# Attention over heads on one Trainium2 core: two tiles of 128 tokens softened with one set of operations

## The reference

```python
qkv = jnp.einsum('bsm,mhd->bshd', x, Wqkv) + bqkv        # 16 heads, 48 = 3 x 16
q, k, v = jnp.split(qkv, 3, axis=-1)                     # [b, s, h, 16]: seq_len = q.shape[-2] = 16 heads
scores = jnp.einsum('...hqd,...hkd->...hqk', qb, kb) / jnp.sqrt(jnp.float32(d))
scores = jnp.where(mask == 0, -1000000000.0, scores)     # mask: lower triangle over the heads
w = jax.nn.softmax(scores, axis=-1)
ob = jnp.einsum('...hqk,...hvd->...hqd', w, vb)          # k and v are separate labels
y = jnp.einsum('bshd,hdm->bsm', attn, Wout) + bout
```

## Time and profile before

| what | value |
|---|---|
| time, median of 3 runs | 434.84 us (433.45 to 437.3) |
| the profiled execution's own time | 432.32 us |
| its span in the profile | 430.5 us |
| mean granted TensorE clock | 0.96 of full speed |
| instructions | 6336 |

### The profile page before, as it was taken

How to read it: one execution, slowest core, us unless ns; L and a number is a source line. 1 busy time by engine, 2 the same in 40 slices (tenths; PEclk the granted TensorE clock), 3 DMA queues, 4 the chain that set the end, 5 groups by cost and what they waited for, 6 DMA issues and landing times.

```text
span 430.5 us, 6336 instructions
## 1 busy us (share of the span) xinstructions
PE 385.0 (89%) x2132; PEld 185.6 (43%) x2132; DVE 320.1 (74%) x503; ACT 233.1 (54%) x444; POOL 149.6 (35%) x159
## 2 busy tenths in 40 slices
PE   2999797989999999999999999898798688977696
PEld 1645342222222222222222354676576356545475
DVE  6638699888878888788887244577689989899643
ACT  2146232667776777868777865533254153553332
POOL 4024305997000000000000001345668678967143
PEclk9999897999999999999999999999899979898889
DMA  7608993950000000000000000000000000000001
GB/s 208 226 3 210 246 249 62 181 106 2 0 3 0 1 0 1 0 1 0 1 0 2 1 2 2 2 2 0 2 1 2 0 0 2 24 0 2 24 2 49
DMA packets 12644, 17.42 MB, mean 40 GB/s; under 512 B 4391, under 2 KB 10443, under 8 KB 11950
## 3 DMA queue, kind: packets, MB, share of 16 engines
q1 hardware_dynamic: 10862, 15.95, 15.3%
q10 hardware_dynamic: 1760, 1.18, 0.9%
HBM read 12.73 MB, written 4.19 MB: 39 GB/s over the span
## 4 chain that ended last, share of the span: by engine, by line
PE 65%; DVE 19%; ACT 5%; DMA 4%; issue 4%; POOL 1%; SPq 1%; ACTq 0%; DVEq 0%
PE ps L1223 15%; PE ps L1209 13%; PE ps L1185 12%; PE ps L1356 7%; DVE s_wide L1034 3%; PE ps L1345 3%; DVE xn L892 3%; DVE mx L931 2%; PE ps L1330 2%; PE ps L1131 2%; DVE pack L1023 2%; DVE stats L875 2%; DMA pack<-q_parts 2%; ACT pbuf L781 1%; PE ps L1391 1%
## 5 line engine op out<-in xcount | busy, mean ns | idle before, releaser
L931 DVE TENSOR_REDUCE mx<-ps 128x1 f32<-128x1024 f32 x128 | 151.0, 1220 | 30.5 <-PE ps L1185 29.8
L781 ACT ACTIVATE pbuf<-ps 128x512 f32<-128x512 f32 x256 | 135.8, 603 | 52.3 <-PE ps L1209 51.5
L1185 PE MATMUL ps<-pack 112*128 (+1 forms) x256 | 79.1, 392 | 4.6 <-DMA pack<-q_parts 2.7
L1209 PE MATMUL ps<-pack 115*128 (+1 forms) x256 | 81.8, 386 | 0.8 <-ACT pbuf L781 0.8
L620 POOL TENSOR_TENSOR rstd<-rstd,minus_half 128x2 f32<-128x2 f32 x16 | 12.1, 756 | 192.8 <-DVE rstd L882 192.7
L1223 PE MATMUL ps<-pbuf,v_slot 128*32 128x512 f32 x512 | 68.2, 604 | 2.0 <-ACT pbuf L781 0.9
L1209 PEld LDWEIGHTS ps<-pack 115*128 (+1 forms) x256 | 21.2, 97 | 80.6 <-issue 60.9
L1356 PE MATMUL ps<-w_nat,pack 128*128 128x256 bf16 x384 | 54.1, 288 | 1.8 <-POOL pack L657 1.8
L669 POOL TENSOR_TENSOR pbuf<-wT 128x1024 f32<-128x1024 f32 (+3 forms) x32 | 49.8, 1574 | 8.4 <-ACT wT L832 8.4
L657 POOL TENSOR_TENSOR pack<-pack 128x256 bf16<-128x256 f32 x64 | 42.0, 666 | 24.2 <-DVE pack L1023 24.2
L1023 DVE TENSOR_TENSOR pack<-pack 128x256 f32<-128x256 f32 x64 | 35.1, 556 | 16.8 <-ACT pack L826 16.6
(11 more groups left out here) (112 smaller groups left out, 383.2 us busy)
## 6 DMA issues: line engine op xcount, KB each, us to landing
pack<-q_parts SPq DMA_DIRECT2D x6, 384.0 KB, 13.9
w_nat<-in_L_ffn_w_dram SPq DMA_DIRECT2D x2, 1024.0 KB, 6.6
k_parts<-parts SPq DMA_DIRECT2D x2, 768.0 KB, 7.4
q_parts<-parts SPq DMA_DIRECT2D x4, 384.0 KB, 9.0
pack<-k_parts SPq DMA_DIRECT2D x4, 384.0 KB, 7.2
pack<-k_parts SPq DMA_DIRECT2D x2, 768.0 KB, 9.1
x_res<-in_L_attn_a_x_dram SPq DMA_DIRECT2D x4, 256.0 KB, 3.6
out_dram<-x_res SPq DMA_DIRECT2D x4, 256.0 KB, 2.1
```

The lines of the kernel that those rows point to most:

```text
L781: act.activation(pbuf[:, c % 2, j, :], ps[:, b, :], ACT.Exp).then_inc(drained[b], 1)
L931: dve.tensor_reduce(mx[:, par, k:k + 1], ps[:, b:b + 2, :].rearrange("p b k -> p (b k)"), AX_X, ALU.max) \
L1185: ins = pe.matmul(ps[:, b + n, :], q_group[0:ROWS, qh, at, j, P * qt:P * qt + P].rearrange("p g t -> p (g t)"), k_group[0:ROWS, at, j, HAL ...
L1209: pe.matmul(ps[:, b, :], k_group[0:SROWS, at, j, P * c:P * c + P].rearrange("p g t -> p (g t)"), q_group[0:SROWS, qh, at, j, :].rearrange( ...
```

## The change

Tiles 2p and 2p + 1 are softened together. The steps vs, soft, exp_heads and wv exist once for each pair p, in the planned place of the odd tile, with operations over both tiles: the mask over 128 numbers, maximum, subtraction, exp, sum and outer product over 512, reciprocal and product over 32. vs.p computes both tiles' summed values, in one bank, with the same matmuls as before. o, o_out, bo_y and res stay per tile; those of the even tile move to directly before those of the odd tile, 0.9 apart in the plan. The planned start of tile 6 moves from 81.69 to 84.0 and that of tile 7 from 89.69 to 90.5. The first sum of each even tile from tile 2 on also waits until the last pair has been shifted, a semaphore of VectorE's own; the qk copy waits for GpSimd's products of tile t - 3 instead of that tile's drained bank.

In the sorted list TensorE's part becomes, for example: qk.5, bo_y.3, two y_parts, lnt.3.1, y.1.0, qk.6, h.1.1.0, vs.2, h.1.1.1, h.1.1.2, qk.7, h.1.1.3, o.4, and later vs.3, y.1.1, o.6, h.1.2.0, o.7, bo_y.6, bo_y.7, h.1.2.1, h.1.2.2, lnt.3.3.

```diff
-HEADS_AT = (39.0, 47.93, 56.72, 63.93, 72.93, 78.84, 81.69, 89.69)
-HEADS_LAG = (0.0, 2.7, 8.6, 9.89, 11.1, 11.36, 13.07, 13.77, 14.1, 15.1)
+HEADS_AT = (39.0, 47.93, 56.72, 63.93, 72.93, 78.84, 84.0, 90.5)
+HEADS_LAG = (0.0, 2.7)
+SOFT_LAG = (8.6, 9.89, 11.1, 11.36)
+HEADS_OUT_LAG = (13.07, 13.77, 14.1, 15.1)
+HEADS_OUT_STEP = 0.9
...
         if t % 2:
-            yield from pair_slots(3, t // 2, at + HEADS_LAG[-1])
+            p = t // 2
+            for lag, kind in zip(SOFT_LAG, ("vs", "soft", "exp_heads", "wv")):
+                yield at + lag, (kind, p)
+            for i in (0, 1):
+                for lag, event in zip(HEADS_OUT_LAG, (("o", "b", 2 * p + i), ("o_out", "b", 2 * p + i), ("bo_y", 2 * p + i),
+                                                      ("res", 2, 2 * p + i))):
+                    yield at + lag + HEADS_OUT_STEP * i, event
+            yield from pair_slots(3, p, at + HEADS_OUT_LAG[-1] + HEADS_OUT_STEP)
...
             def qk_out(t):
                 if t >= 3:
-                    is_drained(act, ("vs", t - 3))
+                    act.wait_ge(products, QUADS * (t - 2))
...
-            def exp_heads(t):
-                act.wait_ge(shifted, t + 1)
-                act.activation(probs[:, t % 2, :, :], probs[:, t % 2, :, :], ACT.Exp, scale=SCALE).then_inc(exped, 1)
+            def exp_heads(p):
+                act.wait_ge(shifted, p + 1)
+                act.activation(probs, probs, ACT.Exp, scale=SCALE).then_inc(exped, 1)
...
                 dve.wait_ge(products, taken[0])
+                if quad == QUADS - 1 and t and t % 2 == 0:
+                    dve.wait_ge(shifted, t // 2)
...
+            def soften(p):
 
                 dve.wait_ge(reduced, taken[0])
+                is_filled(dve, ("vs", p))
+                hmax = beside_v_sums(p, 1)
+                link(dve.tensor_tensor(s_diag, s_diag, causal[:, :, :].unsqueeze(1).broadcast_to([P, 2 * QUADS, 4, 4]), ALU.add))
+                link(dve.tensor_reduce(hmax, s_raw, AX_X, ALU.max))
+                dve.tensor_tensor(probs, s_raw, hmax.unsqueeze(3).broadcast_to([P, 2, H, H]), ALU.subtract).then_inc(shifted, 1)
+
+            def head_outputs(p):
+
+
+                dve.wait_ge(exped, p + 1)
+                hsum = beside_v_sums(p, 2)
+                link(dve.tensor_reduce(hsum, probs, AX_X, ALU.add))
+                link(dve.reciprocal(w_sum[:, :, :], hsum))
+                link(dve.tensor_tensor(w_sum[:, :, :], hsum, w_sum[:, :, :], ALU.mult))
+                n = number["o", "b", 2 * p]
+                for i in (0, 1):
+                    is_filled(dve, outs[n - 2 + i])
+                dve.tensor_tensor(o_norm.rearrange("p r (h n) -> p r h n", h=H),
+                                  w_sum[:, :, :].unsqueeze(3).broadcast_to([P, 2, H, HD]),
+                                  beside_v_sums(p, 0).unsqueeze(2).broadcast_to([P, 2, H, HD]), ALU.mult) \
+                    .then_inc(drain_sem(("vs", p)), 1)
...
                 else:
-                    is_drained(pe, ("vs", t))
+                    is_drained(pe, ("vs", t // 2))
...
+            def heads_v_sums(key):
+
+                p = key[1]
+                if p == 0:
                     pe.wait_ge(vsum_ready, 1)
+                to_fill(pe, key)
+                for i in (0, 1):
+                    t, out = 2 * p + i, beside_v_sums(p, 0)[:, i, :]
+                    pe.matmul(out, ones[0:1, :], b_vsum[:, :], start=True, stop=False)
+                    for d in range(DC):
+                        ins = pe.matmul(out, xT[:, d, P * t:P * t + P], w_vsum[:, d, :], start=False, stop=(d == DC - 1))
                 ins.then_inc(fill_sem(key), 1)
```

More of the change, by code:

```diff
@@ L195, in heads_slots @@
     for t, at in enumerate(HEADS_AT):
[L196 to L199, removed]
+        for lag, kind in zip(HEADS_LAG, ("qk", "qk_out")):
+            yield at + lag, (kind, t)
         for n in range(QUADS):
@@ L220, in tail_events @@
     for t in range(TT):
-        assert all(place["sum", t, quad] < place["soft", t] for quad in range(QUADS))
+        for quad in range(QUADS):
+            assert place["sum", t, quad] < place["soft", t // 2]
+            assert t < 2 or place["soft", t // 2 - 1] < place["sum", t, quad]
     for k in (1, 2, 3):
@@ L340, in build @@
         s_raw = s_wide[:, :, 0:H * H].rearrange("p r (i j) -> p r i j", i=H)
-        s_diag = s_wide[:, :, :].rearrange("p r (q x) -> p r q x", q=QUADS)[:, :, :, 0:4 * H] \
-            .rearrange("p r q (i j) -> p r q i j", i=4)[:, :, :, :, 0:4]
+        s_diag = s_wide[:, :, :].rearrange("p r (q x) -> p (r q) x", q=QUADS)[:, :, 0:4 * H] \
+            .rearrange("p q (i j) -> p q i j", i=4)[:, :, :, 0:4]
         w_out = sb("w_out", [P, DC, D])
@@ L371, in build @@
         rsum = sb("rsum", [P, 2, H])
-        w_sum = sb("w_sum", [P, H])
+        w_sum = sb("w_sum", [P, 2, H])
         w_vsum = sb("w_vsum", [P, DC, HD])
@@ L457, in is_filled, with beside_v_sums @@
             return ps[:, b, :]
-        def beside_v_sum(t, n):
-            return ps[:, uses["vs", t][0], HD * n:HD * n + HD]
+        def beside_v_sums(p, n):
+            return ps[:, uses["vs", p][0], 2 * HD * n:2 * HD * n + 2 * HD].rearrange("p (i h) -> p i h", i=2)
         def is_drained(eng, key):
@@ L1032, in head_scores @@
                 dve.wait_ge(products, taken[0])
+                if quad == QUADS - 1 and t and t % 2 == 0:
+                    dve.wait_ge(shifted, t // 2)
                 _, _, terms = factors(t, quad, slot)
                 dve.tensor_reduce(s_raw[:, t % 2, i, 0:nj], terms, AX_X, ALU.add).then_inc(reduced, 1)
-            def soften(t):
+            def soften(p):
                 dve.wait_ge(reduced, taken[0])
[L1039 to L1060, removed]
+                is_filled(dve, ("vs", p))
@@ L1394, in heads_qk @@
                 ins.then_inc(fill_sem(key), 1)
-            def heads_v_sum(key):
-                t = key[1]
-                if t == 0:
+            def heads_v_sums(key):
+                p = key[1]
+                if p == 0:
                     pe.wait_ge(vsum_ready, 1)
[L1401 to L1404, removed]
+                to_fill(pe, key)
[4 more added lines that the diff above has]
+                        ins = pe.matmul(out, xT[:, d, P * t:P * t + P], w_vsum[:, d, :], start=False, stop=(d == DC - 1))
                 ins.then_inc(fill_sem(key), 1)
             tail = {"w": w_transposed, "ao_t": o_to_tokens, "o": o_to_features, "ao_y": project_o,
-                    "lnt": transpose_pair, "h": hidden, "y": ffn_out, "qk": heads_qk, "vs": heads_v_sum,
+                    "lnt": transpose_pair, "h": hidden, "y": ffn_out, "qk": heads_qk, "vs": heads_v_sums,
                     "bo_y": project_o}
```

## The result

The changed kernel is slower: 447.67 us (median of 4 runs, 443.47 to 450.04) against 434.14 us (median of 4), ratio 1.0316 with a 95% interval of 1.0274 to 1.0359. The forecast was 433.8 us with a range of 428.5 to 439.0. The profiled execution took 448.01 us, with a span of 446.2.

What follows compares the result with a forecast made beforehand. TensorE was taken as the bound on average, in the tail waiting mostly for VectorE's layer norms. Step offsets of -0.4 us and -0.6 for a table load made -1.0: from 434.84 to 433.8 us, range 428.5 to 439.

Steps and rivals of the forecast that it cites:

- Saving on VectorE: Softening on VectorE: about 5.5 us less work over four pairs, plus 1 to 2 us from fewer mask stalls.
- ScalarE, 7.7 and 0.8 us: Softening on ScalarE: 7.7 us off through fewer exp and gelu table loads, some 0.8 us from fewer exps.
- Step (a): TensorE up to h.1.0.0 at 345 us: two norms about as before, offset 0, bounds -1.1 and +1.1 us.
- Step (b): TensorE up to lnt.3.1: idle there grows from 1.2 to about 2.6 us; offset +0.4, bounds -1.0 and +2.
- Step (c): TensorE up to o.4: waits some 3 us for the pair's outer product; offset -0.9 us.
- Step (d): TensorE up to lnt.3.2: tile 6's outer-product wait and softening gone, norm hangs on bo_y.5; offset -3.0 us.
- (e): TensorE up to o.6: vs.3 and joint softening longer; offset -1.6 us at the low clock, -2.4 at the high.
- (f): TensorE up to lnt.3.3: more work before the last norm; offset 0.0 at the low clock, -0.8 us at the high.
- bunched output drops the clock: Rival: longer waits at lnt.3.1 and o.4, each followed by the low clock; about +5 us, 440 us; chance 0.13.
- VectorE's saving reaches the end: Rival: tail gains at o.4 and lnt.3.2 last, high clock follows; some -6.3 us, 428.5 us; chance 0.25.
- Joined operations cost double: Rival: operations over 512 numbers cost twice those of 256, VectorE saves only stalls; 434 to 436 us; chance 0.04.
- The two signs of being wrong: Prediction wrong if lnt.3.3 comes 3 us or more before 407.5, or a pair's operations cost what two tiles' did.

Runs made afterwards that it cites:

- experiment 2: Kernel before with only the new starts of tiles 6 and 7 and the changed waits, every tile softened by itself: ratio 1.0011.
- experiment 13: Tiles softened singly in their own places, even outputs directly before odd ones, odd outputs and layer norm where the kernel before has them: ratio 1.0126 to that kernel.
- experiment 5: Tiles softened singly in their own places, even outputs directly before odd ones, odd outputs and layer norm 0.9 later: 447.10 us, ratio 1.0289 to the kernel before.
- experiment 1: Changed kernel's order of steps, but each softening operation done tile by tile over 256 numbers instead of 512: 450.32 us, ratio 1.0392 to the kernel before.
- experiment 6: Changed kernel with both tiles' outputs and the layer norm planned 0.9 earlier, joint softening unchanged: ratio 1.0251 to the kernel before.
- experiment 7: Only tiles 0 and 1 softened jointly, outputs bunched as in the changed kernel, tiles 2 to 7 each by itself: ratio 1.0157 to the kernel before.
- experiment 9: Changed kernel with GpSimd waiting for the normalised pair after one power alone, at norm.3.0: ratio 1.0209 to the kernel before.
- experiment 14: Changed kernel with outputs planned 0.9 earlier and GpSimd waiting for the normalised pair at norm.3.0: ratio 1.0274 to the kernel before.

## Why the prediction was wrong

In steps from the kernel before, each uncertain by 0.4 to 0.8 per cent: new starts 0.1%; even outputs bunched +1.2%, shifted by 0.9 +1.6% (experiments 2, 13, 5); softening of the even tile late +1.0% (experiment 1 against 5); operations joined -0.8% (the change against experiment 1). The steps run from one end to the other, so that they add up to the measured 3.2% proves nothing. They also depend on their order. With the outputs 0.9 earlier, joint softening costs 1.25% (experiment 6 against 13, uncertain by 0.6), with 11.1 us of waits for outer products against 7.4, and not 0.3; and going back by 0.9 gives only 0.65%, not 1.6. What is shown is that the order of the steps costs 3 to 4% (experiments 1 and 5) and that joined operations don't. The savings were sized rightly, the order was not.

- **What bounds it:** read rightly. The large item of TensorE's waits was the norms, and the change made that item 7.8 us larger.
- **Saving on VectorE, 5.5 us and 1 to 2 of stalls:** the operations fell from 22.6 to 16.4 us (the sums of their groups), 6.2 with the mask's stalls. Of single terms, only the reciprocal was off: 0.358 us for 32 numbers against 0.258 for 16, where 0.27 had been taken. But the engine's busy time fell by 1.3 only: stalled norms gave 4.1 us back (L892's group of 18 had 15.2 us, L902's has 19.3).
- **ScalarE, 7.7 and 0.8 us:** 8.2 measured.
- **Step (a), 0 with bounds of 1.1:** this step failed first, by 6.9 us. It took "the two norms about as before" and followed TensorE and VectorE alone; the two copies that change places in ScalarE's list, and the products behind them, stand nowhere in it. norm.3.0 began 4.2 us behind (the second projection, a qk at the low clock with 3.45 us for four matmuls that took 1.98, and norm.2.3 held for 2.57 us instead of 0.74) and then took 2.8 us longer than before. In the profiles with pair 0 shifted by 0.9 and no gate (the changed kernel, experiments 1, 5 and 7) tile 3's copy comes first and the norm takes 4.31 to 4.32 us; in those without it (the kernel before, experiments 2, 6 and 13) it takes 1.55 or 1.56. Why TensorE got the low clock at that qk stays open: the wait ahead of it (1.25 us) is hardly longer than before (1.10).
- **Step (b), +0.4:** +1.1 measured, with 3.04 us of wait where 2.6 had been forecast. Right in kind.
- **Step (c), a gain of 1.3 (from +0.4 to -0.9):** 1.9 gained, right in kind: 3.98 us of wait at o.4 against "some 3".
- **Step (d), -3.0 forecast, a loss of 2.1 instead of a gain of 2.1 from (c) on:** this step failed next. It said that the layer norm then hangs on bo_y.5 and gave that no price. From the start of o.4 to the end of bo_y.5 TensorE took 9.6 us (388.72 to 398.34), where the same matmuls take about 5.9 at the high clock (an estimate from the rows of the kernel before), as the 3.98 us wait was followed by the low one. VectorE, which was to be the engine freed, waited 3.48 and 2.65 us for the two projections meanwhile:

```profile
394.98 0.42 DVE L987 TENSOR_TENSOR x_res<-ps,x_res 128x256 f32<-128x256 f32 x1 [3.48 <-PE ps L1341]
...
398.38 0.42 DVE L987 TENSOR_TENSOR x_res<-ps,x_res 128x256 f32<-128x256 f32 x1 [2.65 <-PE ps L1341]
```

- **Steps (e) and (f), -1.6 and 0:** 2.6 and 4.2 us lost where 1.4 and 1.6 had been forecast. The two projections of 1.13 us each took 2.08 there:

```profile
415.22 2.08 PE L1341 MATMUL ps<-w_out,parts 128*128 128x256 f32 x4
...
417.55 2.08 PE L1341 MATMUL ps<-w_out,parts 128*128 128x256 f32 x4
```

- **The rivals:** "bunched output drops the clock" was the nearest, with 0.13 of chance, but its 440 us are still 7.7 short. It named the two waits, and both came; but it charged them once each and saw no wait ahead of lnt.3.0. The profile has five waits of 3 us and more, four of them followed by a low stretch; the 3.04 us before lnt.3.1, which it had counted, was not. "VectorE's saving reaches the end" fell: VectorE's share from 382 to 402 us fell to 13.6 of 20, and nothing came of it. "Joined operations cost double" fell: 0.69 us for 512 numbers against 0.42 for 256.
- **Range:** the bounds of (a) and (b) moved each step by itself. In a chain of engines that wait for each other a late step makes the next one late and slow as well, and both ends should have been carried on. The two signs of being wrong that it named, an earlier lnt.3.3 and dear operations, could not have shown this loss.

What stays open: how the 1.6% of the shift is divided between the blocked norm.3.0 and the lost cover of later pairs. Experiments 9 and 14 have intervals too wide or effects that overlap. The profiled executions of experiments 5 and 13 hint at half each (5.0 us apart at lnt.3.0, 10.0 at lnt.3.3), but they lie further apart (12.8 us) than the 7 us of the ratios. How much the late softening of the even tile costs by itself is open too.

## What to carry to other kernels

Joining the operations of two tiles saves fixed costs, but it also joins their results: what stood between the first tile's output and the second's now stands behind both. Before joining, follow the step that needs both results (here a layer norm) and count what newly lies in front of it, on every engine, and at the low clock where a long wait precedes it. Then compare the sorted lists of every engine, also of those with time to spare: a copy that changed places on ScalarE, busy half the time, let GpSimd's products in ahead of the norm. Where such a chain already has small waits between full engines, a saving of 14 us of work on two engines was worth some 3 us here, and the order that it needs cost 17.

## What the hardware showed that was not expected

Two operations of VectorE can be held by three operations of GpSimd in a row: 4.31 us for 0.73 us of work. Yet to hold GpSimd back for them cost 6 to 7 us in the kernel before (ratio 1.0164). And the granted clock followed the waits, but not each of them: 0.75 and 0.74 in the windows with the waits of 6.63 and 3.98 us, 1.00 in the one between, which holds the wait of 3.04. A reciprocal costs 0.1 us for 16 numbers more, where the product of the same size costs 0.02 (0.192 against 0.174 us).
